# A lag of five items in place of four in a software-pipelined attention and expert kernel

## The reference

```python
q = (x @ Wq.T + bq)...; k = ...; v = ...            # 16 heads of 8
scores = einsum('bhqd,bhkd->bhqk', q, k) / sqrt(hd)
attn = softmax(where(causal, scores, -inf))
out = einsum('bhqk,bhkd->bhqd', attn, v) @ Wo.T + bo
top_val, top_idx = top_k(x @ gate_w.T, 2); top_w = softmax(top_val)
y = sum over the two experts of top_w * (x @ We[e])
result = x + attention(layernorm(x)) + experts(layernorm(x))
```

## Time and profile before

| what | us |
|---|---|
| median of three runs | 518.96 |
| lowest and highest of them | 516.93 and 520.93 |
| the profiled execution | 520.78 |
| span of that execution in the trace | 518.6 |

### The profile page before, as it was taken

One profiled execution on the slowest core, in us unless ns is written; L12 is line 12 of the kernel. 1 busy time (PEld: TensorE's weight loads), 2 busy tenths in 40 slices (PEclk: granted clock), 3 DMA queues, 4 the chain that ended last, 5 costly groups with the idle time before them and its releaser, 6 DMA issues.

```text
span 518.6 us, 17312 instructions
## 1 busy us (share of the span) xinstructions
PE 481.6 (93%) x6274; PEld 395.7 (76%) x6274; DVE 420.5 (81%) x1111; ACT 397.5 (77%) x1062; POOL 346.0 (67%) x561
## 2 busy tenths in 40 slices
PE   2549799999999999999999999999999999999994
PEld 1427688888887888888888888878787888888762
DVE  5897688888888888888888898888888898887711
ACT  3645678878887888788888888878887888887763
POOL 7265647777777677777777777767767678754443
PEclk9999989999999999999999999999999999999997
DMA  4755746655547456655465566654646566650000
GB/s 125 197 130 123 188 100 158 153 134 144 143 121 159 121 151 158 152 140 142 114 166 134 142 148 149 159 149 112 162 120 152 126 153 152 149 140 13 15 13 21
DMA packets 64281, 67.79 MB, mean 131 GB/s; under 512 B 6828, under 2 KB 59180, under 8 KB 59484
## 3 DMA queue, kind: packets, MB, share of 16 engines
q1 hardware_dynamic: 64196, 66.68, 52.0%
HBM read 44.90 MB, written 21.23 MB: 128 GB/s over the span
## 4 chain that ended last, share of the span: by engine, by line
PE 77%; DMA 7%; ACT 6%; DVE 4%; issue 3%; SPq 1%; POOL 0%; DVEq 0%; ACTq 0%; POOLq 0%
PE m L841 19%; PE oT_ps L911 15%; PE scoreT_ps L887 10%; PE score_ps L867 10%; DMA qstack<-mT 6%; PE scoreT_ps L892 6%; PE score_ps L861 5%; PE m L1000 3%; PE m L953 3%; ACT upper L549 2%; PE m L1018 2%; ACT probs L499 2%; PE m L926 2%; PE m L1025 1%; PE m L962 1%
## 5 line engine op out<-in xcount | busy, mean ns | idle before, releaser
L625 DVE TENSOR_REDUCE negmax<-score_ps 128x2 f32<-128x512 f32 (+1 forms) x384 | 250.1, 678 | 52.3 <-PE score_ps L867 51.9
L499 ACT ACTIVATE probs<-scoreT_ps 128x512 f32<-128x512 f32 x384 | 216.8, 603 | 78.9 <-PE scoreT_ps L892 41.8
L394 POOL TENSOR_TENSOR fours<-lower,upper 128x512 f32<-128x512 f32 x64 | 81.7, 1277 | 61.4 <-ACT upper L549 61.4
L841 PE MATMUL m<-we_hl,xnT_hl 128*128 128x512 f32 x384 | 114.4, 420 | 0.0
L867 PE MATMUL score_ps<-kstack,qstack 72*128 72x128 bf16 (+1 forms) x1024 | 104.4, 224 | 5.6 <-DVE negmax L625 5.5
L887 PE MATMUL scoreT_ps<-qstack,kstack 123*128 123x128 bf16 (+1 forms) x1024 | 101.8, 221 | 7.6 <-DMA qstack<-mT 5.7
L911 PE MATMUL oT_ps<-probs,vaug 128*32 128x256 f32 (+1 forms) x2048 | 97.7, 331 | 1.3 <-ACT probs L499 1.2
L887 PEld LDWEIGHTS scoreT_ps<-qstack,kstack 123*128 123x128 bf16 (+1 forms) x1024 | 70.0, 98 | 21.6 <-issue 16.5
L911 PEld LDWEIGHTS oT_ps<-probs,vaug 128*32 128x32 f32 x2048 | 57.6, 110 | 30.7 <-ACT probs L499 1.9
L549 ACT ACTIVATE upper<-m,weight 128x128 f32<-128x128 f32 x256 | 73.3, 376 | 9.3 <-PE m L841 9.3
L867 PEld LDWEIGHTS score_ps<-kstack,qstack 72*128 72x128 bf16 (+1 forms) x1024 | 72.5, 100 | 8.4 <-DVE negmax L625 7.8
(11 more groups left out here) (81 smaller groups left out, 651.1 us busy)
## 6 DMA issues: line engine op xcount, KB each, us to landing
kstack<-scratch SPq DMA_DIRECT2D x93, 192.0 KB
scratch<-parts SPq DMA_DIRECT2D x64, 192.0 KB, 2.4
qstack<-scratch SPq DMA_DIRECT2D x62, 192.0 KB
qstack<-scratch SPq DMA_DIRECT2D x31, 256.0 KB
x_sb<-in_x SPq DMA_DIRECT2D x32, 128.0 KB, 2.3
scratch<-parts SPq DMA_DIRECT2D x32, 128.0 KB, 1.9
out<-out_sb SPq DMA_DIRECT2D x32, 128.0 KB, 3.3
qstack<-mT SPq DMA_DIRECT2D x64, 8.0 KB, 2.1
```

The lines of the kernel that those rows point to most:

```text
L394: g.tensor_tensor(fours[:, :, q, :], lower[:, :, q, :], upper[:, :, q, :], ALU.add).then_inc(pool_sum, 1)
L499: a.activation(o, i, ACT.Exp, scale=SCALE).then_inc(act_exp, 1)
L625: v.tensor_reduce(o, score_ps[n % 2][:].rearrange("p (h k) -> p h k", h=w), axis=AX.X, op=ALU.max, negate=True).then_inc(dve_max, 1)
L841: ins = tn.matmul(o, l, r, start=first, stop=l is low)
```

## The change

`LAG` becomes 5: a sequence's second pass now begins at step 5 of the slot after its first pass, so that items 0 to 6 are done in steps 5 to 11 and items 7 to 11 in steps 0 to 4 of the next slot, on TensorE and on ScalarE. The special places of the last sequence's values go: its groups 0 and 1 are done at step 3 and groups 2 and 3 at step 6 of slot 33, as for every other sequence. The number of instructions, their operands and the buffers stay as they are.

```diff
-LAG = 4
+LAG = 5
...
                     if n == 1 and has(s, PRE):
                         pe.wait_ge(act_upper, upto(fin, per=2))
                         project(pre)
-                    if s == NSEQ and n in (9, 11):
-                        values(mix, (9, 11).index(n))
-                    if s == NSEQ + 1 and n in (2, 4):
-                        values(fin, (2, 4).index(n) + 2)
-                    if n == 3 and has(s, -2) and s <= NSEQ:
+                    if n == 3 and has(s, -2):
                         values(fin, 0)
                         values(fin, 1)
...
-                    if n == 6 and has(s, -2) and s <= NSEQ:
+                    if n == 6 and has(s, -2):
                         values(fin, 2)
                         values(fin, 3)
```

## The result

The changed kernel takes 515.74 us (median of 13 executions, 512.39 to 518.22) against 519.73 us of the kernel before (13 executions, 516.93 to 522.56). The ratio is 0.992 with a 95% interval of 0.990 to 0.995: 4.0 us faster by the medians, about 0.8%. The profiled execution of the change took 512.65 us (span 510.5) and was among the shortest of its kernel, while that of before (520.78, span 518.6) lies above its median. The two traces differ by 8.1 us, twice as much as the medians.

The account below looks back on a forecast made before the run. TensorE, busy for 93% of the span, was taken as the bound, with short waits for the maxima's DMA. Fill 0.47, full slots 3.3 and drain 0.8 sum to 4.6 us: 520.78 - 4.6 = 516.2 us, range 514 to 520.

Parts of the forecast that it names:

- Full slots: Eight TensorE waits for the maxima's landing, costing 4.0 us, mostly go as item 0 stands 0.47 us later: gain 3.3 us.
- 0.73 would stay: Of the delays from the eight full-slot waits for the maxima, 0.60 and 0.13 us were expected to remain.
- Values of group 3: At step 6 they wait for the last exponential, now at step 4; 0.70 us of cover, so no cost.
- slower rival: Group 3's values wait for the last exponential in every slot; 30 slots lose 22 us in all: 538; chance 0.08.
- Slot 2: Landing of the maxima fixed, TensorE going on at 62.95, wait and slower clock kept; standing two items further gives 0.47 us.
- a rival: Slot 2's long wait goes too, saving 2.92 + 0.15 us and at least 1.1 of slow clock: 512.0; chance 0.10.
- The drain: Last sequence's group 0 and 1 bursts no longer precede the experts of steps 9 and 11: 0.8 us, between nothing and 1.8.
- the finish behind it is the same: Behind the last sequence's group 3 burst, expected at 509.14 in place of 509.97, the finish was taken as unchanged.
- The spread of the runs: Read as full-slot waits coming and going; with fewer left, the changed kernel's runs should lie close together.
- The sum: 0.47 + 3.3 + 0.8 = 4.6 us off the profiled execution's 520.78 gives 516.2, taken for the median too.

Follow-up runs that it names:

- early stacks: Stack loads of sequence 2 issued at the end of slot 0: on the change 511.20 us, on the kernel before 514.48, with a lag of six 508.74.
- later maxima: Writes of the maxima issued behind the next input's load: on the change 517.66 us (ratio 0.995), on the kernel before 525.50 (1.010).
- lag alone: The change with the last sequence's values kept apart in four single bursts: 518.65 us, ratio 0.996 to the kernel before.
- lag of six: The change with `LAG = 6`, keeping its two bursts: 511.19 us, ratio 0.983 to the kernel before.
- bursts alone: The change with `LAG = 4`, so only the last sequence's two bursts differ from the kernel before: 517.68 us, ratio 0.994.
- input's load first: The change with SyncE's load of the next input ahead of the two `mT` writes: 515.66 us, ratio 0.991 to the kernel before.
- later stacks: Stack loads of sequence 3 issued in slot 2 behind its maxima, here with a lag of six: 513.21 us, ratio 0.987 to the kernel before.

## Why the prediction was right, point by point

The forecast was 516.2 us and no difference over 1%; it is 515.74 and 0.8%. The mechanisms of the two main terms, full slots and drain, were right. What was wrong is that slot 2 would keep its slower clock, and what the spread of the runs comes from.

- *Full slots (3.3 us):* 3.76 in the traces, and 3.07 in the pair with the early stacks. Packed slots stayed at 14.40, the waits went, and slots 3 to 30 hold hardly anything above 26 x 14.40 and the two last, shorter ones (14.23 and 13.50), 402.1 in all. The experiments with later maxima confirm the cause. That 0.73 would stay was too much for this execution; the one with the lag alone kept more.
- *Values of group 3 (no cost, 0.70 us of cover):* right to the hundredth, and the lag of six shows that even 0.2 us is enough. The slower rival had nothing to it.
- *Slot 2 (start fixed at 62.95, its wait and the slower clock kept):* the landing was as fixed as said, 62.81, and the wait 2.56. But in the profiled execution the clock did not fall behind it, which made slot 2's gain 1.88 in place of some tenths. I had put this into a rival as coming only with the wait; it came without. The row of before showed one execution of an event that happens in some and not in others.
- *The drain (0.8 us):* 1.02 at the last burst, close to it, and the same again in the pair with the early stacks. Behind it I wrote "the finish behind it is the same", and the profiled execution took 1.19 us less there than that of before, the same matmuls at a higher clock. But the other traces put most of that down to the two executions and leave some 0.4 us to the drain (0.10 in the pair with the early stacks), so the term itself was nearly right. The bursts alone show 1.5 and 1.2, from one execution.
- *The spread of the runs:* I read it as the full slots' waits coming and going and expected the change's runs to lie close together. They spread over 5.8 us, as before's do (5.6), so that reading was wrong. With the wait of slot 2 gone they spread over 3.7 us at a lag of five and 2.3 at a lag of six, but over 1.4 at a lag of six with that wait still there, and all three numbers come from five or six executions, not thirteen. So slot 2 may hold a part of the spread and the start of slot 1 another; that either holds most of it is not shown. The record has the mean granted clock of each execution: the five of the change at 0.995 to 0.998 took 512.39 to 515.74 us, the eight at 0.975 to 0.981 took 514.84 to 518.22. The spread goes with the clock, then, but only one of the thirteen has a trace, and where in the others the clock differed stays open.
- *The sum:* 4.6 us were meant against the profiled execution of before. That pair of executions differs by 8.1 us, since the change's had neither slower clock; the medians differ by 4.0. So 516.2 lies near the median for a reason that is in part luck: a sum too small for the pair was taken from an execution 1 us slower than the median. Where neither execution has slot 2's wait the sum fits: 4.6 us in the traces with the early stacks, 3.3 by their medians.

## What to carry to other kernels

When one engine is packed but for short waits on one transfer, look at how far the consumer stands behind the issue in program order: a step of lag that costs no work can buy the missing half microsecond, until something else (here the values behind the last exponential) has no cover left. A long wait in the fill is worth more than its length when a slower clock can follow it (2.92 us of wait cost 4.6 us in slot 2 of the kernel before); look for idle stretches of the queues ahead of it rather than putting its loads off, since a burst that is only moved makes the next one wait. And in a drain, order the work so that what the busiest follower waits for comes first, and leave to the end what can be hidden in its waits.

## What the runs showed of the hardware

A wait of TensorE is followed by the lower clock in some executions and not in others, and its length does not decide it here: the granted clock fell behind 2.92 us of wait in the kernel before (0.59) and behind 2.85 with the lag alone (0.70 in 64.00 to 66.60), but stayed at 1.00 behind 2.56 in the change, 3.02 with the input's load first and 3.45 at a lag of six with the later stacks. In the drain, behind idle times of 0.2 to 0.95 us between short bursts, it was 0.60 over the last 8.63 us of the kernel before, and 0.69 to 0.88 in the five kernels with the change's drain.

A small write lands late behind a burst of loads: the 8 KB writes of the maxima land 5.8 us after their issue behind slot 2's stack loads, 1.9 us with these loads moved away.

And the recorded clock of the start does not tell the level there: four matmuls of the first pass took 0.61 us at about 36 us in both rows below, where the record says 1.00 for 36 to 38 us in the change and 0.50 in the kernel with the early stacks; in full slots such a group takes 0.39. What the record does tell is when the quick level comes. In the five traces of fourteen that say 0.50 for 36 to 38 us such groups are down to 0.40 by 41 to 44 us, in the nine that say 1.00 only by 47 to 49.

```profile
36.51 0.61 PE L867 MATMUL score_ps<-kstack,qstack 72*128 72x128 bf16 x4 [1.37 <-DVE negmax L625]
```

```profile
36.07 0.61 PE L865 MATMUL score_ps<-kstack,qstack 72*128 72x128 bf16 x4 [1.38 <-DVE negmax L623]
```
